# An encoder with a mixture of experts on one core: epsilon as a constant column, coefficient matmuls padded to full rows, the selector rounded by GpSimd, and the order of two waits

## The chip, the cores and the metric

The kernel runs on one core of a Trainium2 chip. The metric is the device time of one execution in microseconds (us). The engines are PE (TensorE, matmuls), DVE (VectorE), ACT (ScalarE), POOL (GpSimd) and SP (SyncE, here only for transfers). They run their own instruction lists in order and wait for each other through semaphores.

## The reference

There are 16 sequences of 256 tokens with 128 features. Each goes through the same work:

```
mod = silu(c) @ wmod                      # shifts, scales and gates, per sequence
h = layernorm(x) * (1 + ca) + sa
y = sqrt(128) * h + positions
for 4 layers:
    n = layernorm(y, ln1); q, k, v = n @ Wq + bq, n @ Wk + bk, n @ Wv + bv
    y = y + linear_attention(q, k, v) @ Wo + bo        # 16 heads of 8, elu + 1
    n = layernorm(y, ln2); y = y + relu(n @ W1 + b1) @ W2 + b2
x = x + ga * layernorm(y, lnf)
h = layernorm(x) * (1 + cb) + sb
coef = the two largest of softmax(h @ router), zero for the other six experts
x = x + gb * (sum over experts of coef * expert(h) + shared(h))
```

A layernorm divides by the root of the variance plus 1e-5. An expert is silu(h @ gate) * (h @ up) @ down with 64 hidden features. Everything is float32; the larger products are made of high and low parts in a rounded float32 format.

## The kernel before

**Chains.** Four sequences run at a time, as chains A, B, C and D, and four steps (loop variable `i`) do all 16. A chain's residual is `b.x`, 128 partitions of 2 tiles x 128 features. The pairs AB and CD run half a layer apart: in phase `n` of a step, one pair is in the attention half of a layer and the other in the feed-forward half. Phases 2 to 6 have the same shape; phases 7 to 9 also hold the end of the encoder, the routing and the experts, with the next step's first layer between them. The last step has no such neighbour.

**Order.** It is written out by hand, one list per engine. Each helper (`move`, `squares`, `rstd`, `scale`, `transposes`, ...) waits for the semaphores it needs and adds one to its own when it is done.

**The normalisation inside the encoder** (norms 1 to 9 of a chain). Weights are prepared so that the residual has mean zero, so the variance is the mean of squares. `move` (L941 to L947, DVE) adds a product from PSUM to `b.x`; it waits for PE's semaphore first and then for POOL's `biased`. `squares` (L406 to L416, ACT) squares each tile with a scale of 128^-0.5 and lets the accumulator sum it into `b.ms`. `rstd` (L646 to L656, POOL) adds epsilon to `b.ms`, giving `b.ve`, and raises that to -0.5, giving `b.rstd`. `scale` (L881 to L894, DVE) multiplies `b.x` by it into `b.xn` (127 of its 128 columns; the last is a constant 1). `transposes` (L1336 to L1342, PE) turns `b.xn`. The norms 0 and 10 use DVE's mean and variance `b.mv` instead, with the same `rstd`.

**The coefficients.** `route` (DVE) leaves two rounded parts of the eight coefficients, `b.parts`, 16 columns a tile. `coef_transposes` (L1440 to L1446, PE) makes 16 rows of them, `coefs` (L442 to L445, ACT) copies them as `b.coefT`, and `spread` (L1448 to L1454, PE) multiplies a slice of `sel_hi` with them, so that every hidden feature's row holds its expert's coefficient. `weigh` (L1038 to L1043, DVE) multiplies by that; it waits for the product before it and then for `spread`. Each chain does two transposes and two pairs of spread matmuls in a step.

**The start.** SP fetches the constants, the selector and the biases, then waits for the modulation. POOL's memsets, its transfers of `wo`, `w2` and the output biases, and four `rstd` come first in its list, then it waits for the modulation rows `M`. The selector `sel` is rounded into `sel_hi` by DVE at the end of its start list (`spreading_ones`, L831 to L833). `less_w2_means` (ACT) uses `eqk` of chain `l` as scratch for layer `l`.

All matmuls go through the helper on line 1305.

Of the kernel before, what the change touches and what calls it, by code (L numbers as in the profile page):

```python
# [39 lines left out]
P = 128  # L40
# [29 lines left out]
S_ROWS = PARTS * EXPERTS  # L70
SPREAD = (2, 2, 4, 8)
# [22 lines left out]
def selectors():  # L94

    k = np.zeros((S_ROWS, CH * P), np.float32)
    for c in range(CH):
        for m in range(P):
            k[2 * c + m // DE + EXPERTS * np.arange(PARTS), c * P + m] = 1
    return k  # L100
# [17 lines left out]
def program(nc, x_in, Wq, bq, Wk, bk, Wv, bv, Wo, bo, W1, b1, W2, b2, ln1_s, ln1_b, ln2_s, ln2_b, lnf_s, lnf_b,  # L118
# [3 lines left out]
    with ctx:  # L122
# [15 lines left out]
        sel_hi = sb("sel_hi", [S_ROWS, CH * P], F32R)  # L138
        sel = sb("sel", [S_ROWS, CH * P])
# [43 lines left out]
        for c in range(CHAINS):  # L183
# [3 lines left out]
            b.x = sb("x" + n, [P, TILES, D])  # L187
# [10 lines left out]
            b.zi = sb("zi" + n, [P, TILES, D])  # L198
# [26 lines left out]
            b.parts = sb("parts" + n, [P, TILES, PARTS, EXPERTS], F32R)  # L225
            b.coefT = sb("coefT" + n, [S_ROWS, T], F32R)
# [9 lines left out]
            b.s_rstd = sig("rstd", 2 * NORMS)  # L236
# [30 lines left out]
        A, B = AB  # L267

# [50 lines left out]
        def _(sync):  # L319
# [6 lines left out]
            sync.dma_start(sel[:, :], select).then_inc(s_sel, 16)  # L326
# [29 lines left out]
        def _(act):  # L356
# [49 lines left out]
            def squares(b, i, n):  # L406

                if n == 1:
                    act.wait_ge(b.s_centred.sem, b.s_centred.value(i, 2))
                else:  # L410
                    act.wait_ge(b.s_moved.sem, b.s_moved.value(i, n))
                for t in range(TILES):
                    unused = b.zi[:, t, :] if n == 1 else b.eq[:, t * P:(t + 1) * P]
                    last = act.activation(unused, b.x[:, t, :], ACT.Square, scale=float(D) ** -0.5,  # L414
# [27 lines left out]
            def coefs(b, i):  # L442
                act.wait_ge(b.s_eps.sem, b.s_eps.of(EXPERT_PS, "coefT", i))
                act.activation(b.coefT[:, :], b.ps[0:S_ROWS, 1, 0:T], ACT.Copy)\
# [36 lines left out]
            squares(a[1], 0, 2)  # L481
            less_w2_means(3, 4)
# [129 lines left out]
        def _(pool):  # L612
# [14 lines left out]
            pool.wait_ge(s_const, 10)  # L627
# [18 lines left out]
            def rstd(b, i, n):  # L646

                if 0 < n <= LAST:
                    pool.wait_ge(b.s_squares.sem, b.s_squares.value(i, n))
                    var = b.ms[:, :]  # L650
                else:
                    pool.wait_ge(b.s_moments.sem, b.s_moments.value(i, 1 if n == 0 else 2))
                    var = b.mv[:, :, 1]
                pool.tensor_tensor(b.ve[:, :], var, epsilon[:, :], ALU.add).then_inc(b.s_rstd.sem, 1)  # L654
                pool.wait_ge(b.s_rstd.sem, b.s_rstd.value(i, 2 * n + 1))
# [23 lines left out]
            rstd(f[1], 0, 0)  # L679
            pool.wait_ge(s_k, 32)  # L680
# [105 lines left out]
        def _(dve):  # L786
# [44 lines left out]
            def spreading_ones():  # L831
                dve.wait_ge(s_sel, 16)
                dve.tensor_copy(sel_hi[:, :], sel[:, :]).then_inc(s_ones, 1)  # L833

# [46 lines left out]
            def scale(b, i, n):  # L881

                dve.wait_ge(b.s_rstd.sem, b.s_rstd.value(i, 2 * n + 2))
# [57 lines left out]
            def move(b, i, n):  # L941

                ps = (b.s_wops, b.s_w2ps)[(n - 1) % 2]
                dve.wait_ge(ps.sem, ps.value(i, (n - 1) // 2 + 1))
                dve.wait_ge(b.s_biased.sem, b.s_biased.value(i, n + 1))
# [117 lines left out]
            dve.wait_ge(s_const, 10)  # L1063
# [38 lines left out]
            spreading_ones()  # L1102
# [200 lines left out]
        def _(pe):  # L1303
# [30 lines left out]
            pe.wait_ge(s_const, 10)  # L1334
# [105 lines left out]
            def coef_transposes(b, i):  # L1440
                pe.wait_ge(b.s_route.sem, b.s_route.value(i, b.s_route.per))
                pe.wait_ge(b.s_units.sem, b.s_units.of(EXPERT_UNITS, "product0", i))
                for t in range(TILES):
                    last = pe.transpose(b.ps[0:S_ROWS, 1, t * P:(t + 1) * P],
                                        b.parts[:, t, :, :].rearrange("p k e -> p (k e)").bitcast(F32), ident)
# [229 lines left out]
```

## Time and profile before

| | |
|---|---|
| median of 3 runs | 657.01 us (656.51, 657.01, 661.86) |
| the profiled execution | 657.81 us |
| its span, first to last instruction | 656.0 us |
| PE busy | 594.7 us, 91% of the span |
| DVE busy | 473.0 us, 72% |
| ACT busy | 380.4 us, 58% |
| POOL busy | 298.3 us, 45% |
| transfers in the first 16.4 us | 275 GB/s, the DMA engines 92% busy |
| mean granted TensorE clock | 0.966 of full; 0.61 from 16 to 66 us |

Busy time of one engine says little about the end, since the engines overlap. The chain of waits is followed back from the last instruction, at each step to what released it. The timeline lists instructions with their start and duration, and in brackets how long the engine was idle before and for whom. The ends of matmuls are modelled, so the pace of a row of matmuls is read from their starts.

### The profile page before, as it was taken

To read this page: it belongs to the slowest core of one execution; us is meant where nothing else is said; L and a number is where in the kernel's file an instruction comes from. 1 tells how busy PE (TensorE), PEld (TensorE's weight loads), DVE (VectorE), ACT (ScalarE), POOL (GpSimd) and SP (SyncE) were. 2 spreads that over 40 slices of the span, in tenths; PEclk is the share of its full clock that TensorE was granted. 3 is DMA by queue.
4 is the path that set the end of the run, shared out by engine and by line. 5 is a ranking of instruction groups with operands and counts; after the bars stand their busy time and mean duration, and the time that the engine had idled before them with its cause. 6 is when DMAs were issued, how large, how long until landed. Compare 5 with 4: busy or idle time off the path is not lost.

```text
span 656.0 us, 12768 instructions
## 1 busy us (share of the span) xinstructions
PE 594.7 (91%) x4378; PEld 538.4 (82%) x4378; DVE 473.0 (72%) x1441; ACT 380.4 (58%) x1344; POOL 298.3 (45%) x549
## 2 busy tenths in 40 slices
PE   2766999998999999997999999998999999998987
PEld 0255999997788999996788999997788999997776
DVE  6684666668997656669998565668998566668783
ACT  0657566654576665664576656664576665665431
POOL 5248544456443444455443354456443354445310
PEclk9566999999999999999999999999999999999999
DMA  9803300000000000000000000000000000000000
GB/s 275 289 3 101 121 2 1 1 1 1 1 16 18 0 1 2 1 1 0 2 17 11 8 1 1 1 2 0 2 17 2 17 1 2 1 1 1 1 16 17
DMA packets 10416, 15.79 MB, mean 24 GB/s; under 512 B 848, under 2 KB 7580, under 8 KB 10096
## 3 DMA queue, kind: packets, MB, share of 16 engines
q1 hardware_dynamic: 6192, 9.79, 4.7%
q0 software_dynamic: 1008, 2.83, 1.5%
q10 hardware_dynamic: 3152, 2.36, 1.3%
q8 instruction: 35, 0.57, 0.3%
q14 instruction: 29, 0.24, 0.1%
HBM read 12.84 MB, written 2.14 MB: 23 GB/s over the span
## 4 chain that ended last, share of the span: by engine, by line
PE 57%; DVE 17%; POOL 9%; ACT 9%; issue 5%; DMA 2%; DVEq 1%; SPq 0%; POOLq 0%
PE psC L1305 15%; PE psA L1305 15%; PE psD L1305 12%; PE psB L1305 9%; POOL rstdC L656 2%; POOL rstdA L656 2%; POOL rstdB L656 2%; ACT eqkA L414 1%; PE psB L1341 1%; ACT eqkC L414 1%; DVE xnB L886 1%; ACT eqkB L414 1%; PE psC L1341 1%; DVE xnA L886 1%; PE psA L1341 1%
## 5 line engine op out<-in xcount | busy, mean ns | idle before, releaser
L414 ACT ACTIVATE eqkC<-xC 128x128 f32<-128x128 f32 x64 | 19.3, 301 | 36.0 <-DVE xC L946 35.9
L654 POOL TENSOR_TENSOR veA<-msA,epsilon 128x2 f32<-128x2 f32 x36 | 7.0, 196 | 65.1 <-ACT eqkA L414 61.2
L656 POOL TENSOR_TENSOR rstdA<-veA,neghalf 128x2 f32<-128x2 f32 x44 | 33.6, 764 | 3.4
L656 POOL TENSOR_TENSOR rstdC<-veC,neghalf 128x2 f32<-128x2 f32 x44 | 33.6, 763 | 3.4
L654 POOL TENSOR_TENSOR veB<-msB,epsilon 128x2 f32<-128x2 f32 x36 | 7.3, 203 | 60.8 <-ACT eqkB L414 59.7
L654 POOL TENSOR_TENSOR veD<-msD,epsilon 128x2 f32<-128x2 f32 x36 | 7.1, 198 | 57.4 <-ACT eqkD L414 56.8
L654 POOL TENSOR_TENSOR veC<-msC,epsilon 128x2 f32<-128x2 f32 x36 | 7.1, 198 | 55.4 <-ACT eqkC L414 48.8
L656 POOL TENSOR_TENSOR rstdD<-veD,neghalf 128x2 f32<-128x2 f32 x44 | 30.7, 699 | 3.4
L656 POOL TENSOR_TENSOR rstdB<-veB,neghalf 128x2 f32<-128x2 f32 x44 | 30.6, 695 | 3.4
L1305 PE MATMUL psC<-w,H 128*128 128x128 f32 x256 | 31.5, 276 | 0.0
L1305 PE MATMUL psD<-w,H 128*128 128x128 f32 x256 | 31.4, 276 | 0.0
L1305 PE MATMUL psB<-w,H 128*128 128x128 f32 x256 | 31.4, 276 | 0.0
L1305 PE MATMUL psA<-w,H 128*128 128x128 f32 x256 | 31.2, 275 | 0.0
L414 ACT ACTIVATE eqkA<-xA 128x128 f32<-128x128 f32 x64 | 19.2, 301 | 20.5 <-DVE xA L946 20.5
L1305 PEld LDWEIGHTS psC<-w,H 128*128 128x128 f32 x256 | 30.0, 192 | 0.8 <-ACT H L435 0.7
L1305 PEld LDWEIGHTS psD<-w,H 128*128 128x128 f32 x256 | 30.1, 192 | 0.2
L1305 PEld LDWEIGHTS psA<-w,H 128*128 128x128 f32 x256 | 30.0, 192 | 0.0
L1305 PEld LDWEIGHTS psB<-w,H 128*128 128x128 f32 x256 | 29.8, 192 | 0.0
L435 ACT ACTIVATE H<-psD 128x512 f32<-128x512 f32 x32 | 19.0, 593 | 12.9 <-PE psD L1305 12.4
L1305 PE MATMUL psC<-xhiC,w_hi 128*128 128x256 f32 x64 | 20.9, 326 | 3.6 <-DVE xloC L909 3.6
L392 ACT ACTIVATE xhiB<-psB 128x256 fp32r<-128x256 f32 x32 | 12.4, 389 | 19.9 <-PE psB L1341 19.9
L414 ACT ACTIVATE eqkD<-xD 128x128 f32<-128x128 f32 x64 | 19.2, 305 | 7.9 <-DVE xD L946 7.4
(495 smaller groups left out, 2376.7 us busy)
## 6 DMA issues: line engine op xcount, KB each, us to landing
M<-modulation_rows SPq DMA_DIRECT2D x1, 2560.0 KB, 11.2
out<-X SPq DMA_DIRECT2D x16, 128.0 KB, 1.9
M<-modulation_rows SPq DMA_DIRECT2D x2, 640.0 KB, 5.3
M<-modulation_rows SPq DMA_DIRECT2D x1, 1280.0 KB, 8.8
M<-in_attn_W ACTq DMA_DIRECT2D x1, 1024.0 KB, 15.5
w<-in_attn_W POOLq DMA_DIRECT2D x1, 1024.0 KB, 11.6
X<-in_attn_x_in ACTq DMA_DIRECT2D x1, 512.0 KB, 4.7
wm<-in_wmod SPq DMA_DIRECT2D x1, 384.0 KB, 6.4
```

The source lines that it names most:

```text
L392: act.activation(b.x_hi[:, :], b.ps[:, n % 2, 0:T], ACT.Copy).then_inc(b.s_xT.sem, 1)
L414: last = act.activation(unused, b.x[:, t, :], ACT.Square, scale=float(D) ** -0.5, accum_out=b.ms[:, t:t + 1])
L435: act.activation(b.h[:, 2 * k:2 * k + 2, :], b.ps[:, k, :].rearrange("p (c t) -> p c t", t=T), ACT.Relu).then_inc(b.s_h.sem, 1)
L654: pool.tensor_tensor(b.ve[:, :], var, epsilon[:, :], ALU.add).then_inc(b.s_rstd.sem, 1)
L656: pool.tensor_tensor(b.rstd[:, :], b.ve[:, :], neghalf[:, :], ALU.pow).then_inc(b.s_rstd.sem, 1)
L886: dve.tensor_tensor(dst[:, :, 0:width], b.x[:, :, 0:width], b.rstd[:, :].unsqueeze(2).to_broadcast([P, TILES, width]), ALU.mult)\
L1305: return pe.matmul(o, lhsT, rhs, start=start, stop=stop)
L1341: last = pe.transpose(b.ps[:, n % 2, t * P:(t + 1) * P], src[:, t, :], ident)
```

## The change

It does five things.

- The residual of each chain becomes `b.xe` with 129 columns a tile; the last is the constant sqrt(128 x 1e-5). `squares` reads all 129, so that epsilon is in the sum, and `rstd` of norms 1 to 9 is the power alone. Its unused output goes to a 129-column view.
- `b.parts` becomes the first 16 of 128 columns, `b.columns`, the rest zero. The coefficient transposes, `b.coefT`, the selector and so the spread matmuls have 128 rows. The selector in memory has 128 rows, 112 of them zero.
- The selector is fetched into the `eqk` scratch of chain D and rounded by POOL after its four first `rstd`, no longer by DVE. ACT waits for that before `less_w2_means(3, 4)`.
- In `move` the two waits change places.
- POOL has eight more memsets in its start, and the engines wait for 18 instead of 10.

```diff
-            b.x = sb("x" + n, [P, TILES, D])
+            b.xe = sb("x" + n, [P, TILES, D + 1])
+            b.x = b.xe[:, :, 0:D]
...
-            b.parts = sb("parts" + n, [P, TILES, PARTS, EXPERTS], F32R)
-            b.coefT = sb("coefT" + n, [S_ROWS, T], F32R)
+            b.columns = sb("columns" + n, [P, TILES, S_ALL], F32R)
+            b.parts = b.columns[:, :, 0:S_ROWS].rearrange("p t (k e) -> p t k e", e=EXPERTS)
+            b.coefT = sb("coefT" + n, [S_ALL, T], F32R)
...
+        sel = flat(chains[3].eqk[:, :, :])
...
+        def rstds(n):
+            return n + 2 + (n > LAST)
...
-            sync.dma_start(sel[:, :], select).then_inc(s_sel, 16)
+            sync.dma_start(sel, select).then_inc(s_sel, 16)
...
+                unused = b.zie if n == 1 else flat(b.eqk[:, :, :])[:, 0:TILES * (D + 1)].rearrange(
+                    "p (t f) -> p t f", f=D + 1)
                 for t in range(TILES):
-                    unused = b.zi[:, t, :] if n == 1 else b.eq[:, t * P:(t + 1) * P]
-                    last = act.activation(unused, b.x[:, t, :], ACT.Square, scale=float(D) ** -0.5,
+                    last = act.activation(unused[:, t, :], b.xe[:, t, :], ACT.Square, scale=float(D) ** -0.5,
                                           accum_out=b.ms[:, t:t + 1])
...
-                act.activation(b.coefT[:, :], b.ps[0:S_ROWS, 1, 0:T], ACT.Copy)\
+                act.activation(b.coefT[:, :], b.ps[:, 1, 0:T], ACT.Copy)\
...
+            act.wait_ge(s_ones, 1)
             less_w2_means(3, 4)
...
                 pool.memset(b.v[:, :, D:], 1.0).then_inc(s_const, 1)
+                pool.memset(b.columns[:, :, S_ROWS:].bitcast(F32), 0.0).then_inc(s_const, 1)
+                pool.memset(b.xe[:, :, D:], float(np.sqrt(D * EPS))).then_inc(s_const, 1)
...
                 if 0 < n <= LAST:
                     pool.wait_ge(b.s_squares.sem, b.s_squares.value(i, n))
-                    var = b.ms[:, :]
-                else:
-                    pool.wait_ge(b.s_moments.sem, b.s_moments.value(i, 1 if n == 0 else 2))
-                    var = b.mv[:, :, 1]
-                pool.tensor_tensor(b.ve[:, :], var, epsilon[:, :], ALU.add).then_inc(b.s_rstd.sem, 1)
-                pool.wait_ge(b.s_rstd.sem, b.s_rstd.value(i, 2 * n + 1))
+                    pool.tensor_tensor(b.rstd[:, :], b.ms[:, :], neghalf[:, :], ALU.pow).then_inc(b.s_rstd.sem, 1)
+                    return
+                pool.wait_ge(b.s_moments.sem, b.s_moments.value(i, 1 if n == 0 else 2))
+                pool.tensor_tensor(b.ve[:, :], b.mv[:, :, 1], epsilon[:, :], ALU.add).then_inc(b.s_rstd.sem, 1)
+                pool.wait_ge(b.s_rstd.sem, b.s_rstd.value(i, rstds(n) - 1))
                 pool.tensor_tensor(b.rstd[:, :], b.ve[:, :], neghalf[:, :], ALU.pow).then_inc(b.s_rstd.sem, 1)
...
             rstd(f[1], 0, 0)
+            pool.wait_ge(s_sel, 16)
+            pool.tensor_copy(sel_hi[:, :], sel).then_inc(s_ones, 1)
             pool.wait_ge(s_k, 32)
...
-            def spreading_ones():
-                dve.wait_ge(s_sel, 16)
-                dve.tensor_copy(sel_hi[:, :], sel[:, :]).then_inc(s_ones, 1)
...
                 ps = (b.s_wops, b.s_w2ps)[(n - 1) % 2]
+                dve.wait_ge(b.s_biased.sem, b.s_biased.value(i, n + 1))
                 dve.wait_ge(ps.sem, ps.value(i, (n - 1) // 2 + 1))
-                dve.wait_ge(b.s_biased.sem, b.s_biased.value(i, n + 1))
...
-                    last = pe.transpose(b.ps[0:S_ROWS, 1, t * P:(t + 1) * P],
-                                        b.parts[:, t, :, :].rearrange("p k e -> p (k e)").bitcast(F32), ident)
+                    last = pe.transpose(b.ps[:, 1, t * P:(t + 1) * P], b.columns[:, t, :].bitcast(F32), ident)
```

## Rows read from the trace of the kernel before

**Rows 1.** The page, part 4: shares of the chain by engine.
```profile
PE 57%; DVE 17%; POOL 9%; ACT 9%; issue 5%; DMA 2%; DVEq 1%; SPq 0%; POOLq 0%
```
**Rows 2.** Timeline, one phase: start, duration, instruction, [idle before].
```profile
232.03 0.61 PE L1305 MATMUL psA<-wo,guA 128*128 128x128 f32 x4
...
232.68 0.43 DVE L946 TENSOR_TENSOR xA<-psA,xA 128x256 f32<-128x256 f32 x1 [0.84 <-PE psA L1305]
...
233.91 0.20 POOL L654 TENSOR_TENSOR veA<-msA,epsilon 128x2 f32<-128x2 f32 x1 [1.60 <-ACT eqkA L414]
...
234.18 0.90 POOL L656 TENSOR_TENSOR rstdA<-veA,neghalf 128x2 f32<-128x2 f32 x1
...
234.99 0.38 PE L1341 MATMUL psC<-K,xnC 128*128 128x128 f32 x2
235.12 0.42 DVE L886 TENSOR_TENSOR xnA<-xA,rstdA 128x254 f32<-128x254 f32 x1 [0.58 <-POOL rstdA L656]
...
235.60 0.44 PE L1341 MATMUL psA<-K,xnA 128*128 128x128 f32 x2 [0.23 <-DVE xnA L886]
...
235.88 0.42 DVE L909 TENSOR_TENSOR xloC<-psC,xhiC 128x256 fp32r<-128x256 f32 x1
...
236.56 0.28 PE L1305 MATMUL psC<-wqkv_hi,xloC 128*128 128x256 f32 x1
```
**Rows 3.** The chain in order of time: start, duration; first and last of 24.
```profile
71.25 0.92 POOL rstdC L656
...
586.71 0.92 POOL rstdA L656
```
**Rows 4.** Busy time by stretch: length, then PE, PEld, DVE, ACT, POOL.
```profile
295.00:312.00 17.00, 13.43 (x98) 11.69 (x99) 15.53 (x50) 6.61 (x26) 9.41 (x19) 1.00 0.00 0
```
**Rows 5.** Lines 654 and 656: count, ns min/median/max; one of four chains each.
```profile
L654 POOL TENSOR_TENSOR veA<-msA,epsilon x36: 188/196/201, 29.7 to 596.2; 128x2 f32<-128x2 f32 x36
...
L656 POOL TENSOR_TENSOR rstdA<-veA,neghalf x44: 691/702/917, 7.4 to 600.5; 128x2 f32<-128x2 f32 x44
```
**Rows 6.** Separate wait instructions of lines 945 and 1041; timeline, last step.
```profile
L945 DVEq EVENT_SEMAPHORE  x128: 21/21/21, 48.5 to 620.8; - x128
...
L1041 DVEq EVENT_SEMAPHORE  x32: 21/21/21, 171.2 to 646.0; - x32
...
644.43 0.50 PE L1305 MATMUL psD<-coefTD,sel_hi 16*128 16x256 f32 x2
...
645.04 0.69 DVE L1042 TENSOR_TENSOR H<-guD,psD 128x512 f32<-128x512 f32 x1 [1.49 <-PE psD L1305]
```
**Rows 7.** Timeline, DVE in the routing stretch.
```profile
320.79 0.94 DVE L886 TENSOR_TENSOR guD<-xD,rstdD 128x256 f32<-128x256 f32 x1
```
**Rows 8.** Timeline, PE in the routing stretch.
```profile
338.12 0.38 PE L1305 MATMUL psC<-kpC,wg 128*128 128x256 f32 x1
338.34 1.03 PE L1305 MATMUL psD<-kpD,wu 128*128 128x256 f32 x4
...
339.56 0.81 PE L1305 MATMUL psC<-kpC,wu 128*128 128x256 f32 x3
...
347.83 1.03 PE L1305 MATMUL psC<-kpC,wu 128*128 128x256 f32 x4
...
349.76 0.38 PE L1386 MATMUL psA<-K,attA 128*128 128x128 f32 x2
```
**Rows 9.** Timeline, the end of a step: DVE, ACT, POOL.
```profile
346.68 0.19 DVE L932 TENSOR_SCALAR denA<-psA 128x32 f32<-128x32 f32 x1 [0.28 <-PE psA L1305]
...
356.82 0.19 ACT L414 ACTIVATION_READ_ACCUMULATOR ziC<-xC 128x1 f32 x1
...
357.69 0.77 POOL L656 TENSOR_TENSOR rstdC<-veC,neghalf 128x2 f32<-128x2 f32 x1
```
**Rows 10.** Timeline, the start: DVE and POOL.
```profile
57.49 1.22 DVE L833 CAST sel_hi<-sel 16x512 fp32r<-16x512 f32 x1
...
23.47 0.72 POOL L669 TENSOR_TENSOR xA<-M,K 128x256 f32<-128x256 f32 x1 [12.53 <-DMA M<-modulation_rows]
```

More of the change, by code:

```diff
@@ L70 @@
 S_ROWS = PARTS * EXPERTS
+S_ALL = P
 SPREAD = (2, 2, 4, 8)
@@ L94, in selectors @@
 def selectors():
-    k = np.zeros((S_ROWS, CH * P), np.float32)
+    k = np.zeros((S_ALL, CH * P), np.float32)
     for c in range(CH):
@@ L137, in program @@
         pos = K[:, C_POS:C_POS + TILES * D].rearrange("p (t f) -> p t f", f=D)
-        sel_hi = sb("sel_hi", [S_ROWS, CH * P], F32R)
-        sel = sb("sel", [S_ROWS, CH * P])
+        sel_hi = sb("sel_hi", [S_ALL, CH * P], F32R)
         X = sb("X", [P, BATCH * TILES * D])
@@ L197, in program @@
             b.attT = b.gu[:, 1, :]
-            b.zi = sb("zi" + n, [P, TILES, D])
+            b.zie = sb("zi" + n, [P, TILES, D + 1])
+            b.zi = b.zie[:, :, 0:D]
             b.x_hi = sb("xhi" + n, [P, T], F32R)
@@ L235, in program @@
             b.s_squares = sig("squares", LAST)
-            b.s_rstd = sig("rstd", 2 * NORMS)
+            b.s_rstd = sig("rstd", NORMS + 2)
             b.s_normed = sig("normed", NORMS)
@@ L275, in program @@
         s_stored = sem("stored")
+        s_ones = sem("ones")
         s_const = sem("const")
         s_zero = sem("zero")
-        s_ones = sem("ones")
         s_parps = sem("parps")
@@ L626, in _ @@
                                a.rearrange("(a l) n -> a (l n)", a=1).to_broadcast([P, LAYERS * D])).then_inc(s_rest, 16)
-            pool.wait_ge(s_const, 10)
+            pool.wait_ge(s_const, 18)
             def moe_weights():
@@ L881, in scale @@
             def scale(b, i, n):
-                dve.wait_ge(b.s_rstd.sem, b.s_rstd.value(i, 2 * n + 2))
+                dve.wait_ge(b.s_rstd.sem, b.s_rstd.value(i, rstds(n)))
                 if 0 < n <= LAST:
@@ L1062, in _ @@
             fold_matrices()
-            dve.wait_ge(s_const, 10)
+            dve.wait_ge(s_const, 18)
             scale(a[0], 0, 0)
@@ L1101, in _ @@
             scale(a[1], 0, 2)
-            spreading_ones()
             for i in range(STEPS):
@@ L1333, in _ @@
             pe.wait_ge(s_low, 1)
-            pe.wait_ge(s_const, 10)
+            pe.wait_ge(s_const, 18)
             def transposes(b, i, n):
```

## The prediction

> **What bounds the kernel now.** I read the page first. TensorE (PE) is busy 91% of the span, but the chain of waits gives PE only 57%; VectorE (DVE), GpSimd (POOL) and ScalarE (ACT) have 35% of it [rows 1]. Each layer sends a chain through all four, and three kinds of stretch differ in what is last.
>
> In the **phases** PE is nearly full, with one hole in each. The timeline shows why: PE ends an output projection, DVE adds it (move), ACT squares, POOL adds epsilon, POOL takes the power, DVE scales, PE transposes. PE's pair of transposes for C starts at 234.99. A pair of 128-column fp32 matmuls passes in 0.22 here (two of 0.11), so A's pair could start at 235.21; it starts at 235.60, behind xnA [rows 2]. That hole of 0.39 us stands 24 times, six in each of four steps: the chain has 24 such powers with 0.91 to 0.93 us each, the first and the last shown [rows 3].
>
> In the **routing stretch** of a step PE has holes, and DVE is full: 15.53 of 17 us [rows 4]. At the **end** of the last step DVE idles for PE (1.49 us before one addition) [rows 6].
>
> **Epsilon in the squares.** Removed: 4 x 36 = 144 POOL additions, 0.20 us each [rows 5], with 0.07 of issue before the power (233.91 + 0.20, then 234.18): 0.27 off each chain. The additions that read mv stay. Added: a 129th element in 288 squares. No row shows it; bounds are nothing and a nanosecond or two. I take nothing, since the chain covers it no worse than now. A second effect: this power takes 0.90, the median is 0.702 [rows 2, 5], and beside it DVE begins xnC with two operands in SBUF. Begun 0.2 earlier it should be the 0.70 kind; bounds 0 and 0.2.
>
> **The two waits of move.** The late wait goes last in the source, and the trace shows the reverse of an aid. The compiled kernel has a separate semaphore instruction on line 945, 128 times: that is the second wait of the source, while the first sits on the addition. With the first one late, DVE starts 0.04 after PE's modelled end (232.03 + 0.61, then 232.68) [rows 2]. In weigh, too, the second wait (line 1041) is the separate one, and there it is late: PE's pair ends at 644.43 + 0.50 = 644.93, DVE starts at 645.04, 0.11 later [rows 6]. So the swap costs 0.07 wherever PE comes last. Behind it in DVE's queue stand scales and low parts, which move with it. Bounds 0 and 0.1.
>
> **A phase, summed.** Chain: -0.27 - 0.20 + 0.07 = -0.40. xnA starts at 234.72 and ends 0.42 later at 235.14, before PE comes for it at 235.21, so the hole closes. Then something else is late. The third matmul of C's projection needs xloC, which DVE starts at 235.88 after ACT's queue and ends at 236.30; that matmul stands at 236.56 now and could start at 236.34 [rows 2]: **0.22**. If the power stays at 0.90, xnA ends at 235.34, PE starts at 235.38, and it is 0.22 again. The move's 0.07 is inside that slack. 24 x 0.22 = **5.3 us**. Bounds: 0.05 a phase (a further wait right behind) and 0.39.
>
> **Routing, first half.** Three powers of this kind lie on the chain one after the other (chains B, B and D): 3 x 0.27. DVE's guD takes 0.94 where such an operation takes 0.42, because POOL's next addition holds it [rows 2, 7]; that addition also comes 0.27 earlier. Together 1.08. One of the four rests on an overlap and DVE is nearly full, so I take 0.8, four times: **3.2**. Bounds 0.3 and 1.2.
>
> **Coefficient matmuls with full rows.** From the first of four wu matmuls (347.83) to the transposes (349.76) PE does six fp32 matmuls of 256 columns and one pair of 16 rows: 1.93. The fp32 pace is 0.22 (338.12 to 338.34), which leaves 0.61, 0.3 each. The nearest stretch with full rows runs from four such matmuls at 338.34 to the next at 339.56 and has three rounded matmuls of 256 columns inside: 1.22 - 0.88 = 0.34, 0.11 each [rows 8]. Both kinds are fp32r; only the rows differ. So a pair goes from 0.61 to 0.23, near 0.4 less, 32 pairs, 12.2 us of PE. Most of it lies beside DVE's list and is worth nothing there. The 32 coefficient transposes get 128 columns of weights instead of 16, and the copies of coefT write the same 256 elements on more partitions: nothing, the load hides behind the matmul before it; without that cover the bound is 0.1 each.
>
> The Trainium skill speaks against this edit. TensorE: Matmul & The Clock Gate says (Part 2, step 1) that a weight load goes by columns while the row count does not matter, and its table of advice gives a single K=32 matmul the time of a K=128 one. By that the padding would bring nothing. The rows differ from it, and the sum goes by them.
>
> **Routing, second half** (three times, where a step follows). PE gains 0.8 with the first two pairs, and DVE can use part: it idles 0.28 for PE before denA (346.68), and 0.1 to 0.2 more before the weigh behind it. I take 0.47 for both; from there DVE's and ACT's lists run without a break. At their end ACT has C's squares at 356.82 + 0.19 = 357.01, and the last of four powers on POOL, queued behind four additions, starts at 357.69 [rows 9]. Without the additions it starts 0.07 after the squares, at 357.08: 0.61. Together 1.08, taken as 0.9: **2.7**. Bounds 0.4 and 1.5.
>
> **End.** Four pairs for C and D where DVE waits for PE: 4 x 0.4 = **1.6**. Bounds 0 and 2.5 (part of A's and B's pairs too).
>
> **Start.** DVE loses the selector's rounding, 1.22 at 57.49, on the chain [rows 10]; PE still has B's transposes before it, so I count 0.7 of it. Against that POOL rounds a 128x512 tile in a stretch where it idles 12.53 us before 23.47 [rows 10], so its own length is covered; but DVE's modulation steps lie there, and as guD shows, a DVE operation waits while POOL holds the port: up to the copy's whole length, 1.2. Without that idle time it would cost 1.2 on POOL as well. The memsets (some 900 elements a partition, I allow 0.4) come before POOL's weight transfers, and the selector is 256 KB, not 32, ahead of SP's bias transfers: 224 KB more at the 275 GB/s of the first slice is 0.8. Of this 2.4 I expect 0.7 to be seen, the rest hidden by the wait for the modulation rows. ACT's new wait stands late, long after the copy, and costs nothing; were the copy late, the fourth layer's weights and all of ACT's queue would be. Net **0**, bounds -1.1 (all of the rounding, none of the rest) and +1.7 (2.4 - 0.7).
>
> **Sum.** 5.3 + 3.2 + 2.7 + 1.6 = 12.8. The profiled execution took 657.81 (span 656.0), so **645.0**. That execution stands 0.8 above the median of 657.01, inside the spread of the three runs.
>
> **Rivals.** *Gains eaten (0.18).* Right behind each closed hole another wait is late, as xloC already is. Phases 24 x 0.05 = 1.2, routing 4 x 0.3 and 3 x 0.5, end 0.8: 4.7 less, 653.1. For it: DVE's full list. Against: in the phase I find 0.22 before the next wait.
>
> *The padding gives nothing (0.12).* The 0.4 belongs to something other than rows. Left are 5.3, 3.2 and 3 x 0.61: 10.3 less, 647.5. Against: the two stretches differ in nothing else that a row shows. This is the skill's rule at work.
>
> *All of it counts (0.08).* Upper bounds in the phases (9.4), in routing (4.8 and 4.5) and 1.6: 637.5.
>
> *The odd row, slower (0.06).* The residual's rows become 129 floats, so its second tile starts at byte 516, and every move, square, scale and POOL addition reads so. The phase's chain has four of them (move, square, square, scale): from 0.10 extra each the 0.40 is gone. At 0.15 a phase loses 0.2, 4.8 in all; in routing some 14 DVE operations a step on a full engine, 4 x 14 x 0.15 = 8.4; less the 7.5 from routing and end: 663.5. Against: the scale already writes 127 of each 128 elements and takes 0.42 like whole rows [rows 2].
>
> **Numbers.** The forecast's own case gets 0.56. Measurement tells about 1%, 6.6 us, from no change. Faster than 650.4 are the forecast, the padding's rival and the upper case, 0.76, less a little for their spread: 0.74; within 1% 0.19; slower 0.07. The range leaves out most of the upper case and the odd row, and takes in eaten gains: 639.5 to 653.5.
>
> **What the new profile should show.** No addition from ms; powers at 0.70 in the phases; nearly no wait before the transposes, and C's third matmul waiting instead; coefficient matmuls at 0.12; move starting 0.11 after PE's end; the rounding at 57.5 gone from DVE. Wrong would be: longer operations on x, phases as long as now, or a first phase that comes over 1 us later.

## The result

The kernel after took 639.92 us (median of 4 runs, 639.23 to 641.70), against 656.90 for the kernel before beside it: ratio 0.973 (0.970 to 0.975), 17 us faster. The forecast was 645.0, its range began at 639.5: the direction was right, the size 5 us too small. Repeated later with six runs it took 640.6, against 657.5.

The page of the kernel after, busy time by engine and the shares of the chain of waits; the second answers to [rows 1]:

```profile
PE 583.4 (91%) x4378; PEld 538.3 (84%) x4378; DVE 467.9 (73%) x1440; ACT 378.0 (59%) x1344; POOL 265.9 (42%) x414
...
PE 65%; DVE 15%; ACT 10%; issue 4%; POOL 3%; DMA 2%; DVEq 1%; SPq 0%; POOLq 0%
```

POOL fell from 9% to 3% of the chain and PE rose from 57% to 65%. Where did the 17.9 us between the two profiled spans (656.0 and 638.1) go? (By the medians it is 17.0: the profiled execution of the kernel before, 657.81, stands 0.9 above its median.) I cut both traces at the transposes of chain A (the pair psA<-K,xnA), which every phase has, and in each step at those between the two halves of a routing stretch. Differences to the kernel before, us; the columns "column alone" and "padding alone" are experiments, below:

```
stretch                                forecast   after   column alone   padding alone
start, to A's transposes of phase 2       0.0     -2.82      -0.22          +1.11
the phases (forecast for 24)             -5.3     -4.83      -5.22          -0.01
routing, first half, 3 times             -2.4     -4.23      -3.43          -0.50
routing, second half, 3 times            -2.7     -3.77      -0.86          -1.85
last step, from its routing on           -2.4     -2.22      -0.74          -1.33
sum                                     -12.8    -17.87     -10.47          -2.58
of it behind the start (the body)       -12.8    -15.05     -10.25          -3.69
```

The cuts leave 5 phases in the first step and 6 in each of the other three; the 24th lies in the start's row. Two terms are off: the start by 2.8 and routing by 2.9. The phases came 0.5 short and the last step 0.2, which leaves the 5.1. Of that 5.1, 0.9 is the profiled execution's distance from its median, from which the forecast was taken off; the bodies of two profiles of one kernel agree to 0.1, so nearly all of this 0.9 stands in the start's 2.8.

**A phase.** The timeline of the kernel after, the stretch of [rows 2]:

```profile
225.12 0.60 PE L1313 MATMUL psA<-wo,guA 128*128 128x128 f32 x4
...
225.84 0.43 DVE L955 TENSOR_TENSOR xA<-psA,xA 128x256 f32<-128x256 f32 x1 [0.92 <-PE psA L1313]
...
227.07 0.69 POOL L662 TENSOR_TENSOR rstdA<-msA,neghalf 128x2 f32<-128x2 f32 x1 [1.86 <-ACT eqkA L423]
227.21 0.41 DVE L895 TENSOR_TENSOR xnC<-xC,rstdC 128x254 f32<-128x254 f32 x1
...
227.79 0.42 DVE L895 TENSOR_TENSOR xnA<-xA,rstdA 128x254 f32<-128x254 f32 x1 [0.17 <-POOL rstdA L662]
...
228.08 0.38 PE L1349 MATMUL psC<-K,xnC 128*128 128x128 f32 x2
...
228.29 0.41 PE L1349 MATMUL psA<-K,xnA 128*128 128x128 f32 x2
...
228.97 0.42 DVE L918 TENSOR_TENSOR xloC<-psC,xhiC 128x256 fp32r<-128x256 f32 x1 [0.41 <-ACT xhiC L400]
...
229.50 0.34 PE L1313 MATMUL psC<-wqkv_hi,xloC 128*128 128x256 f32 x1
```

The addition is gone and the power takes 0.69. A's transposes follow C's by 0.21, so the hole of 0.39 is closed. Then C's third matmul waits for xloC: from the first output projection to that matmul it is 4.38 now and was 4.53. So of the hole's 0.39 a phase keeps 0.15 to 0.17, not the 0.22 of the working: xloC ends at 229.39 and the matmul starts 0.11 behind it, where the working had 0.04. The length of a phase says the same: from C's transposes to A's of the next phase it was 13.33 (234.99 to 248.32) and is 13.16 (228.08 to 241.24).

**Routing.** The operation that POOL held up for 0.94 [rows 7] takes 0.42. In the second half POOL's last power starts 0.07 behind ACT's squares (346.81 + 0.19), where it started 0.68 behind them [rows 9]; but DVE now waits for a product of PE:

```profile
311.99 0.42 DVE L895 TENSOR_TENSOR guD<-xD,rstdD 128x256 f32<-128x256 f32 x1
...
346.81 0.19 ACT L423 ACTIVATION_READ_ACCUMULATOR ziC<-xC 128x1 f32 x1
...
347.07 0.69 POOL L662 TENSOR_TENSOR rstdC<-msC,neghalf 128x2 f32<-128x2 f32 x1 [0.62 <-ACT ziC L423]
...
347.27 0.42 DVE L1058 TENSOR_TENSOR guC<-psC,M 128x256 f32<-128x256 f32 x1 [0.34 <-PE psC L1313]
```

**The start.** The granted clock (column behind the busy times; 0.50 is 1.2 GHz, 1.00 is 2.4) in slices of 4 us, the kernel before and then the kernel after:

```profile
56.00:60.00 4.00, 3.19 (x14) 2.49 (x13) 3.91 (x6) 2.26 (x8) 4.00 (x5) 0.50 0.02 4
60.00:64.00 4.00, 4.00 (x28) 4.00 (x27) 0.46 (x2) 1.32 (x4) 4.00 (x6) 0.72 0.84 256
```
```profile
56.00:60.00 4.00, 3.86 (x26) 3.57 (x25) 1.82 (x5) 2.68 (x10) 4.00 (x6) 0.73 0.37 86
60.00:64.00 4.00, 4.00 (x36) 4.00 (x35) 1.43 (x5) 2.74 (x7) 4.00 (x7) 1.00 0.88 313
```

PE's timeline shows the moment. Kernel before:

```profile
57.62 0.69 PE L1341 MATMUL psB<-K,xnB 128*128 128x128 f32 x2 [0.46 <-DVE xnB L886]
...
58.32 0.41 PE L1305 MATMUL psD<-wqkv_lo,xhiD 128*128 128x256 f32 x1
59.09 0.58 PE L1305 MATMUL psD<-wqkv_hi,xloD 128*128 128x256 f32 x1 [0.36 <-DVE xloD L909]
...
62.03 0.37 PE L1305 MATMUL psA<-xhiA,w_hi 128*128 128x256 f32 x1
62.24 0.28 PE L1305 MATMUL psA<-xhiA,w_lo 128*128 128x256 f32 x1
62.35 0.28 PE L1305 MATMUL psA<-xloA,w_hi 128*128 128x256 f32 x1
```

Kernel after:

```profile
56.37 0.69 PE L1349 MATMUL psB<-K,xnB 128*128 128x128 f32 x2
...
57.10 0.42 PE L1313 MATMUL psD<-wqkv_lo,xhiD 128*128 128x256 f32 x1
57.32 0.44 PE L1313 MATMUL psD<-wqkv_hi,xloD 128*128 128x256 f32 x1
...
58.00 0.36 PE L1313 MATMUL psD<-wqkv_hi,xloD 128*128 128x256 f32 x1
58.20 0.28 PE L1313 MATMUL psD<-xhiD,wqkv_hi 128*128 128x256 f32 x1
58.32 0.28 PE L1313 MATMUL psD<-xhiD,wqkv_lo 128*128 128x256 f32 x1
```

A matmul of 256 columns starts 0.21 after the one before it at half clock and 0.12 at full. That turn, the clock's rise, stands at 62.2 before and at 58.2 after. B's transposes come 1.25 sooner (57.62, 56.37), and of the 0.77 between the starts of D's second and third matmul (58.32 to 59.09) 0.22 is left.

### The profile page after: what moved, and what is told of

It reads as the page before. It is cut to its first block, busy times and chain, and to the rows that moved or that the text cites. A ratio compares the mean times of both kernels' runs of the same rounds, so it can differ in the third digit from the quotient of the medians.

```text
span 638.1 us, 12632 instructions
## 1 busy us (share of the span) xinstructions
PE 583.4 (91%) x4378; PEld 538.3 (84%) x4378; DVE 467.9 (73%) x1440; ACT 378.0 (59%) x1344; POOL 265.9 (42%) x414
## 4 chain that ended last, share of the span: by engine, by line
PE 65%; DVE 15%; ACT 10%; issue 4%; POOL 3%; DMA 2%; DVEq 1%; SPq 0%; POOLq 0%
PE psB L1313 15%; PE psD L1313 15%; PE psA L1313 15%; PE psC L1313 14%; PE psB L1349 2%; DVE xnB L895 1%; DVE H L1051 1%; PE psA L1349 1%; PE psC L1349 1%; ACT eqkB L423 1%; POOL rstdB L662 1%; DMA wm<-in_wmod 1%; ACT L431 1%; DVEq L885 1%; PE psD L1349 1%
## 5 line engine op out<-in xcount | busy, mean ns | idle before, releaser
L662 POOL TENSOR_TENSOR rstdA<-msA,neghalf 128x2 f32<-128x2 f32 x36 | 25.1, 697 | 68.8 <-ACT eqkA L423 64.9
L662 POOL TENSOR_TENSOR rstdB<-msB,neghalf 128x2 f32<-128x2 f32 x36 | 25.1, 698 | 68.6 <-ACT eqkB L423 67.2
L662 POOL TENSOR_TENSOR rstdD<-msD,neghalf 128x2 f32<-128x2 f32 x36 | 24.9, 692 | 64.6 <-ACT eqkD L423 63.4
L662 POOL TENSOR_TENSOR rstdC<-msC,neghalf 128x2 f32<-128x2 f32 x36 | 25.1, 697 | 59.9 <-ACT eqkC L423 52.2
L423 ACT ACTIVATE eqkC<-xC 128x129 f32<-128x129 f32 x64 | 19.4, 304 | 35.3 <-DVE xC L955 35.3
L423 ACT ACTIVATE eqkA<-xA 128x129 f32<-128x129 f32 x64 | 19.3, 303 | 22.0 <-DVE xA L955 22.0
L955 DVE TENSOR_TENSOR xA<-psA,xA 128x256 f32<-128x256 f32 x32 | 13.5, 423 | 13.9 <-PE psA L1313 13.9
L400 ACT ACTIVATE xhiB<-psB 128x256 fp32r<-128x256 f32 x32 | 12.4, 389 | 18.2 <-PE psB L1349 16.9
L423 ACT ACTIVATE eqkD<-xD 128x129 f32<-128x129 f32 x64 | 19.4, 312 | 6.4 <-DVE xD L955 6.4
L423 ACT ACTIVATE eqkB<-xB 128x129 f32<-128x129 f32 x64 | 19.2, 308 | 5.7 <-DVE xB L955 5.7
L918 DVE TENSOR_TENSOR xloC<-psC,xhiC 128x256 fp32r<-128x256 f32 x32 | 13.6, 424 | 10.7 <-ACT xhiC L400 10.5
## 6 DMA issues: line engine op xcount, KB each, us to landing
M<-modulation_rows SPq DMA_DIRECT2D x1, 2560.0 KB, 11.3
```

The source lines that it names most:

```text
L400: act.activation(b.x_hi[:, :], b.ps[:, n % 2, 0:T], ACT.Copy).then_inc(b.s_xT.sem, 1)
L423: last = act.activation(unused[:, t, :], b.xe[:, t, :], ACT.Square, scale=float(D) ** -0.5, accum_out=b.ms[:, t:t + 1])
L662: pool.tensor_tensor(b.rstd[:, :], b.ms[:, :], neghalf[:, :], ALU.pow).then_inc(b.s_rstd.sem, 1)
L918: dve.tensor_tensor(b.x_lo[:, :], b.ps[:, n % 2, 0:T], b.x_hi[:, :], ALU.subtract)\
L955: dve.tensor_tensor(b.x[:, :, :], b.ps[:, 0, 0:T].rearrange("p (t f) -> p t f", f=D), b.x[:, :, :], ALU.add).then_inc(b.s_moved.sem, 1)
```

## The experiments

Each was timed beside the kernel before on the same chip. The median of the kernel before was 656.9 beside the kernel after, 657.6 beside e1 to e4, 658.4 beside a1 to a4 and 657.5 to 657.9 beside the last group; so times of different groups are compared by their difference to it, and each such difference is known to 1 to 2.5 us. Single runs scatter by 3 us in the kernel after and by 6 in the kernel before (656.3 to 662.6). So I compare the bodies too, the profiled span from A's transposes of phase 2 on. Two profiles of the kernel after have 568.9 and 568.8.

### The parts alone, from the kernel before

**e1, the column.** All of the change's lines on `b.xe`, `zie`, `squares`, `rstds` and `rstd`, and no others:

```diff
-            b.x = sb("x" + n, [P, TILES, D])
+            b.xe = sb("x" + n, [P, TILES, D + 1])
+            b.x = b.xe[:, :, 0:D]
...
-                pool.tensor_tensor(b.ve[:, :], var, epsilon[:, :], ALU.add).then_inc(b.s_rstd.sem, 1)
+                    pool.tensor_tensor(b.rstd[:, :], b.ms[:, :], neghalf[:, :], ALU.pow).then_inc(b.s_rstd.sem, 1)
```


> The kernel before with the constant column alone: 129-column residual and squares, the power straight after the squares, coefficients, selector and waits as before. The theory after the result (each part is worth what its stretch of the two traces shows): 24 phases x 0.2 = 4.8 us, in routing about 0.7 before the first spread matmul and 0.3 at the end of a step, so 3 x 1.0, the last step 0.8, the start nothing: 8.6 less, about 648.4. Rival (holes close only together with the shorter spread pairs): phases as before the theory, routing nothing, about 652. Rival (the recorded sum of the prediction): 5.3 + 3.2 + 3 x 0.61 = 10.3 less, 646.7.

647.3 us, ratio 0.984 (0.982 to 0.986): 10.3 less. The theory's 8.6 missed; the prediction's terms gave the 10.3, but it is otherwise spread: first half 1.14 each, second half 0.29.

**e2, the padding.** 128 rows of columns, `coefT` and selector; DVE rounds.

```diff
-            b.coefT = sb("coefT" + n, [S_ROWS, T], F32R)
+            b.coefT = sb("coefT" + n, [S_ALL, T], F32R)
...
-                    last = pe.transpose(b.ps[0:S_ROWS, 1, t * P:(t + 1) * P],
+                    last = pe.transpose(b.ps[:, 1, t * P:(t + 1) * P], b.columns[:, t, :].bitcast(F32), ident)
```


> The kernel before with the padding alone (128-row coefT, selector and columns; the selector of 256 KB still rounded by DVE from its own buffer). Theory now: PE is what the routing stretch waits for around the spread pairs, so both pairs of a chain count: 0.4 less a pair, less about 0.5 given back once in the first half: 0.85 and 0.95, 1.8 x 3 = 5.4, and 1.4 in the last step: 6.8 less, about 650.2. Rival (the prediction's reading, most of the pairs lie beside DVE's list): 3 x 0.47 + 1.6 = 3.0, about 654. Rival (rows do not matter): 657.

653.2 us, ratio 0.994 (0.992 to 0.996): 4.4 less. The body is 3.7 shorter, near the prediction's 3.0 and not the theory's 6.8. Both parts alone give 10.25 + 3.69 = 13.9 in the body; together they give 15.05. So 1.1 belongs to neither alone.

**e3, the rounding.** POOL rounds the 16-row selector behind its first four `rstd`; DVE doesn't.

```diff
             rstd(f[1], 0, 0)
+            pool.wait_ge(s_sel, 16)
+            pool.tensor_copy(sel_hi[:, :], sel[:, :]).then_inc(s_ones, 1)
...
-            spreading_ones()
```


> The kernel before with one edit: the 16-row selector is rounded by POOL after its first four rstd instead of by DVE at the end of its start list. Theory now: the start's 2.8 us come from here, 0.7 to 1.2 as the rounding leaves DVE's chain at 57.5, the rest as TensorE's clock rises 3 to 4 us sooner: first transposes of C at about 69.5 instead of 72.7, 654.2. Rival (the prediction): 0.7, 656.3. Rival (the clock in the start comes from the memsets, the transfers or the waits of the other parts, not from here): 0 to 0.7 and the clock rows as before.

656.99 us, ratio 0.997 (0.994 to 0.999): 0.6 less, near the prediction's 0.7 and not the theory's 2.8. The wait in front of D's third matmul is gone, B's transposes come no sooner (57.66), the body is the same.

**e4, the waits of move.**

```diff
-                dve.wait_ge(ps.sem, ps.value(i, (n - 1) // 2 + 1))
                 dve.wait_ge(b.s_biased.sem, b.s_biased.value(i, n + 1))
+                dve.wait_ge(ps.sem, ps.value(i, (n - 1) // 2 + 1))
```


> The kernel before with the two waits of move in the other order and nothing else. Theory: DVE's move begins 0.11 instead of 0.04 us after PE's modelled end, 0.07 more on the phase's chain, where the phase's hole is still open: 24 x 0.07 = 1.7, some 658.5 with the routing. Rival (the order is worth nothing, the separate wait costs nothing when it is passed at once either way): 656.9. Rival (the swap helps, because the early wait no longer stands in the way): under 656.

656.8 us, ratio 1.000 (0.998 to 1.001). The 0.07 is there: where DVE waits for PE, `move` starts 0.38 behind the start of PE's last matmul, 0.31 before (median of the same 29 places in both traces). It isn't on the path: the phases are 0.15 shorter in sum, not 1.7 longer. (The body, 584.2 against 583.9, is longer only by a fall of the granted clock to half at 456.3 us in this profile, in a routing stretch that took 0.5 more.) The timeline of e4, a phase:

```profile
232.77 0.61 PE L1305 MATMUL psA<-wo,guA 128*128 128x128 f32 x4
...
234.87 0.41 DVE L886 TENSOR_TENSOR xnC<-xC,rstdC 128x254 f32<-128x254 f32 x1
234.99 0.83 POOL L656 TENSOR_TENSOR rstdA<-veA,neghalf 128x2 f32<-128x2 f32 x1
```

The power starts 0.07 later behind PE's projection than in [rows 2] (2.22 instead of 2.15) and takes 0.83 instead of 0.90: it ends 3.05 behind it in both. Its end stays with DVE's xnC, which starts 2.10 behind the projection in both, and not with its own start.

### The parts taken out of the kernel after

**a1, 16 rows again.**

```diff
-S_ALL = P
+S_ALL = 16
```


> The kernel after with the padding alone undone: columns, coefT, the selector and the transposes have 16 rows again. Theory (what the padding is worth beside the epsilon column, from the traces of the kernel after and of the column alone): first halves 3 x 0.27, second halves 3 x 0.97, last step 1.5: 5.2 more, 645.1. Rival (it is worth what it was worth alone, 4.4): 644.3. Rival (the prediction's term, 3 x 0.47 + 1.6 = 3.0): 642.9.

646.8 us, ratio to before 0.982 (0.978 to 0.985). The body is 573.9 against 568.9: 5.0, the theory's 5.2 (first halves 0.27, second 0.97, last step 1.5).

**a2, DVE rounds again.**

```diff
-            pool.tensor_copy(sel_hi[:, :], sel).then_inc(s_ones, 1)
...
+                dve.tensor_copy(sel_hi[:, :], sel[:, :]).then_inc(s_ones, 1)
```


> The kernel after with the selector (128 rows) fetched into its own buffer and rounded by DVE at the end of its start list. Theory: the hole of 0.55 before D's third matmul at 57 us comes back, and each matmul that then still runs at half clock is lost twice: 0.6 to 1.5 more, 640.5 to 641.4 in the median, and single runs differ by up to 2 us as the clock's rise falls. Rival (the start's 2.8 us are all this edit's): 642.7. Rival (nothing): 639.9.

642.9 us, ratio 0.975 (0.972 to 0.978). The body is 0.2 longer, the profile's start 2.4; by the table below only 0.3 of that is the hole. 642.9 lies near the rival's 642.7, but the kernel before took 1.5 more here than beside the kernel after. By the difference to it (15.5 less, against 17.0) the edit costs 1.5, the upper end of the theory.

**a3, the old order of move's waits.**

```diff
-                dve.wait_ge(b.s_biased.sem, b.s_biased.value(i, n + 1))
                 dve.wait_ge(ps.sem, ps.value(i, (n - 1) // 2 + 1))
+                dve.wait_ge(b.s_biased.sem, b.s_biased.value(i, n + 1))
```


> The kernel after with move's two waits in the order of before. DVE's move should start 0.07 sooner behind PE. Theory: in the kernel after the power no longer ends by DVE's port (there the 0.07 vanished), so it is on the chain, but the phase's hole is closed and C's third matmul waits behind xloC: about 0.02 a phase, 24 x 0.02 = 0.5 less, 639.4, phases at 1.34 instead of 1.2 less than before per six. Rival (hidden): 639.9. Rival (all of the 0.07 counts): 24 x 0.07 = 1.7 less, 638.2.

640.8 us, ratio 0.972 (0.969 to 0.975). The body is 0.2 shorter over the whole run: the phases gain 5.0 instead of 4.8. Nearly all of the 0.07 is hidden. It took 17.6 less than the kernel before, the kernel after 17.0 and 16.9: no difference clear of the noise.

**a4, additions back.**

```diff
+                pool.tensor_tensor(b.ve[:, :], var, epsilon[:, :], ALU.add).then_inc(b.s_rstd.sem, 1)
+                pool.wait_ge(b.s_rstd.sem, b.s_rstd.value(i, 2 * n + 1))
```


> The kernel after with the epsilon column alone undone: 128-column residual, POOL adds epsilon before each power. Theory (the column is worth what it was alone, 10.3): 650.2, phases back to 13.95 us per pair of phases, the power at 0.83 to 0.90 there. Rival (less, since in the routing stretch padding and column share one hole): 8.5 more, 648.4.

653.4 us, ratio 0.991 (0.987 to 0.994). The body is 580.2, that of e2 (580.3), so beside the padding the column is worth 11.3, not 10.3. Neither theory had it more than alone.

### How many rows

```diff
-S_ALL = P
+S_ALL = 64      # and 96
```


> The kernel after with columns, coefT, the selector and the transposes at 64 rows. If the pace of a spread matmul goes with the rows, a pair stands between the 0.61 of 16 rows and the 0.23 of 128, about 0.4, and the second half of a routing stretch loses about half of 0.97; if only full rows are quick, a pair takes 0.6 again and it loses all of it; if anything above 32 rows is quick, nothing is lost.

> The kernel after with 96 rows. With 64 rows the second half of a routing stretch lost 0.98 against 128 rows, as much as with 16 (0.97). If only full rows are quick it is 0.97 again; if the bound lies above 64, nothing to 0.5.

The stretch from the four wu matmuls to the transposes, 1.93 in [rows 8]. In order: the kernels after, with 96, and with 64 rows.

```profile
337.93 1.03 PE L1313 MATMUL psC<-kpC,wu 128*128 128x256 f32 x4
338.60 0.59 PE L1313 MATMUL psD<-coefTD,sel_hi 128*128 128x256 f32 x2
...
339.46 0.38 PE L1394 MATMUL psA<-K,attA 128*128 128x128 f32 x2
```
```profile
338.46 1.03 PE L1313 MATMUL psC<-kpC,wu 128*128 128x256 f32 x4
339.14 0.59 PE L1313 MATMUL psD<-coefTD,sel_hi 96*128 96x256 f32 x2
...
340.00 0.38 PE L1394 MATMUL psA<-K,attA 128*128 128x128 f32 x2
```
```profile
340.88 1.03 PE L1313 MATMUL psC<-kpC,wu 128*128 128x256 f32 x4
341.83 0.50 PE L1313 MATMUL psD<-coefTD,sel_hi 64*128 64x256 f32 x2
...
342.80 0.38 PE L1394 MATMUL psA<-K,attA 128*128 128x128 f32 x2
```

1.53, 1.54 and 1.92: a pair costs 0.4 less at 96 and 128 rows than at 64 and 16. The bodies say the same: 568.9 and 569.0, against 573.7 and 573.9. The 64-row and the 96-row kernel have one run each (645.8 and 640.5), which says little alone.

The weight loads (PEld) show more. The last load of the wu matmuls and the pair's own, the kernel before and then the kernel after:

```profile
348.27 0.19 PEld L1305 LDWEIGHTS psC<-kpC,wu 128*128 128x128 f32 x1
348.79 0.29 PEld L1305 LDWEIGHTS psD<-coefTD,sel_hi 16*128 16x128 f32 x2 [0.33 <-issue]
```
```profile
338.36 0.19 PEld L1313 LDWEIGHTS psC<-kpC,wu 128*128 128x128 f32 x1
338.57 0.41 PEld L1313 LDWEIGHTS psD<-coefTD,sel_hi 128*128 128x128 f32 x2
```

With full rows the pair's first load follows 0.21 behind the one before it, as in a row of equal matmuls; with 16 rows 0.52 behind it, and with 64 rows too. The load itself takes the same: 0.18 us with 16 and 64 rows, 0.19 with 128. That is what the Trainium skill states (TensorE: Matmul & The Clock Gate, Part 2, step 1): the time of a weight load goes by the columns, not by the rows, and the trace agrees. The rival that the prediction made of it, that the padding gives nothing, is false here; with few rows the load only starts later. Whether the few rows bring this, or the change from full rows to few and back, no run separates, since these pairs always stand among matmuls with full rows.

### The start and the clock

**w1 and w2: ten idle products** in PE's wait before the first transposes of phase 1, in the kernels after and before. **w0** is the kernel after itself.

```diff
             pe.wait_ge(s_folded, 2 * LAYERS)
+            for k in range(10):
+                mm(chains[2].ps[:, 1, 0:T], ident, K[:, 0:T])
```


> The kernel after with ten fp32 products of 256 columns more, whose results nobody reads, in PE's wait of 4.75 us before the first transposes of phase 1 (50.0 to 54.7 us). Theory (the start is long because PE runs at half clock from 55 us until it rises, at 58.2 to 63.7 us in the eight kernels seen): the rise comes 2 to 5 us sooner, and each us of it gives back half a us: 1 to 2.5 less than the same kernel without, 637.5 to 639; from run to run less scatter. Rival (that stretch waits for DVE and ACT, the clock is by the way): 640 as before, the rise sooner and holes in PE in its place.

> The kernel before with the same ten idle products at the same place. Theory (clock): the rise, seen at 62.0 us in the profile of before, comes at 56 to 60: 1 to 3 less, about 655; and against the kernel after with the ten products the difference is then the body's 15.1 us (from the first transposes of phase 2 on) plus 0.9 before phase 1 and 0.55 for the rounding's hole: 16.5, so that 1.3 of the 2.8 us of the start are the clock's. Rival (the start's 2.8 have another cause in the change): the difference stays at 17.9.

> The kernel after itself, unchanged, so that its median comes from the same chip and hour as the two before it in this call. Theory: the four runs on record (639.2 to 641.7) had an early rise of the clock; 640.5 here, 17 less than before in the same call. Rival: 639.9.

w1 640.0 us (639.5 to 640.3), w0 640.6 (638.9 to 641.9), w2 656.6 (655.6 to 658.3); ratios 0.973 (0.970 to 0.975), 0.974 (0.971 to 0.976) and 0.998 (0.996 to 0.999). In w1 the clock rises at 53.5 and stays; the products overshoot, the transposes come at 56.4 instead of 55.3, and still nothing is lost. The median gains 0.6, less than the theory's 1 to 2.5; the scatter shrinks from 3.0 to 0.8. (w0 came as expected, 16.9 less than the kernel before.) Between w2 and w1 lie 16.6: the 16.5 of w2's theory, and not the rival's 17.9. In w2's profile the clock rose at 52.7, fell at 59.5 and rose again at 62.9. Before it fell, PE had been idle for 1.07 before B's transposes and then stood idle for 0.80 before D's third matmul. That profile is of the slowest of w2's twelve runs (658.3, mean granted clock 0.974, median of the twelve 0.987), so most of them may not have had the fall; the windows of w2:

```profile
56.00:58.00 2.00, 1.30 (x8) 0.64 (x7) 1.75 (x3) 1.97 (x10) 1.97 (x2) 1.00 0.00 0
58.00:60.00 2.00, 0.83 (x5) 0.62 (x5) 2.00 (x4) 1.01 (x4) 2.00 (x3) 0.88 0.00 0
60.00:62.00 2.00, 2.00 (x10) 2.00 (x11) 0.79 (x3) 0.66 (x2) 2.00 (x3) 0.50 0.35 113
```

**w3 and w4: five such products**, in the kernel after and in e3's.

```diff
+            for k in range(5):
```


> The kernel after with five idle products instead of ten, so that they end (at half clock 4.3 us behind 50.3) before the transposes that wait for DVE. Theory (clock): the rise comes at 53 to 55 us as with ten, the first transposes stand at 55.3 instead of 56.4, and half to all of that 1.1 is gained over the 640.0 with ten: 639.0 to 639.5, scatter under 1 us. Rival (five are too few to raise the clock before the stretch): 640.6 as without them, scatter of 3 us.

> The kernel before with the selector rounded by POOL (no hole at 58 us, in which the clock fell again in the kernel before with ten idle products: it rose at 52.7, was back at half from 59 and rose at 62.8) and five idle products. Theory (the start's 2.8 us are the hole and the clock): with both gone the difference to the kernel after with five is the body's 15.1 and 0.9 before phase 1: 655.0 if that one takes 639.0. Rival (something else of the change shortens the start): it stays near 657.

w3 639.7 us (638.6 to 641.8), ratio 0.973 (0.971 to 0.975); w4 657.4, ratio 0.998 (0.997 to 1.000). The difference is 17.7, where the theory that the hole and the clock make up the start had 16.0; w3's own theory missed too (639.0 to 639.5, scatter under 1; it was 3.2). So the two pairs disagree: 16.6 with ten products, 17.7 with five. Each is known to some 1.5 us, so they don't settle what the hole and the clock are worth together. Two things are seen in the profiles. B's transposes come at 57.90 in w4 and at 56.16 in w3. And w4 has full clock from 54.4 to 57.8, then half, and rises again at 61.3, while w3 has it from 51.9 on and keeps it, though PE idled as long in w3 (1.40 and 0.75) as in w4 (0.97 and 1.07). The longer of w3's waits:

```profile
54.42 0.44 PE L1349 MATMUL psD<-K,xnD 128*128 128x128 f32 x2 [1.40 <-DVE xnD L895]
```

What brought the clock down in w4 and not in w3 is therefore not shown.

All kernels side by side: start of B's transposes in phase 1, the clock's rise behind them, A's transposes of phase 2, the time between first and third, and the body, in us. "Worked out" is 12.82 (r64) plus 0.46 for each us of half clock beyond r64's 1.79; 0.46 is the slope from r64 to a1, (13.92 - 12.82) / (4.19 - 1.79).

```
kernel             B      rise   A, ph.2  between  worked out   body
before           57.62   62.24   72.05    14.43     14.12      583.9   DVE rounds
e1 column        56.45   63.19   71.83    15.38     15.09      573.7   DVE rounds
e2 padding       58.70   63.33   73.16    14.46     14.13      580.3   DVE rounds
e4 waits         57.82   63.72   72.85    15.03     14.71      584.2   DVE rounds
a2               57.44   61.59   71.67    14.23     13.91      569.1   DVE rounds
e3 POOL rounds   57.66   60.06   70.71    13.05     13.10      583.7
after            56.37   58.20   69.23    12.86     12.84      568.9
w0 after again   56.54   58.99   69.66    13.12     13.12      568.8
a1 16 rows       57.15   61.34   71.07    13.92     13.92      573.9
a3 old order     57.03   60.98   70.82    13.79     13.81      568.7
a4 additions     58.06   62.76   72.11    14.05     14.16      580.2
r64              57.41   59.20   70.23    12.82     12.82      573.7
r96              56.47   59.11   69.66    13.19     13.21      569.0
w1, w3           56.88, 56.16: full clock    12.60, 12.62      568.8
```

Three things can be read. The clock's rise falls anywhere from 58.2 to 63.7, and each us of half clock costs 0.46; the slope comes from two kernels, and the others without DVE's rounding lie within about 0.1 of it. Where DVE rounds, the stretch is 0.29 to 0.33 longer than that. And with full clock from the first matmul (w1, w3) it takes 12.6, not the 12.0 of the slope: the first matmuls on D still start 0.22 to 0.23 apart there. So the kernel after's own 12.86 leaves only 0.25 to gain.

## Why the prediction came out 5 us short

**Start, forecast 0, measured -2.82.** (By the medians it is 1.8 to 1.9: 17.0 and 16.9, less the bodies' 15.05 and 15.17.) This step failed most: the prediction put the start at a net of nothing. By the table: B's transposes 1.25 sooner; 2.79 us less of half clock at 0.46, which is 1.28; and the hole 0.31 at most. That makes 2.8. I counted the hole (as 0.7) and set it against the cost of POOL's copy, the memsets and the larger transfer. B's transposes came no later by them in e3 (57.66, with POOL's copy) and sooner in the kernel after; only e2, with memsets and transfer, has them later (58.70), in the profile of its slowest run. I had left out two things. First, the additions stand in the start's chain too. From DVE's addition to B, 50.67, to B's transposes, 57.62, it is 6.95; in e1 6.36 (50.09 to 56.45). Two additions with their issue stood there; the kernel before, then e1:

```profile
54.08 0.20 POOL L654 TENSOR_TENSOR veD<-msD,epsilon 128x2 f32<-128x2 f32 x1 [0.63 <-ACT ziD L414]
54.36 0.69 POOL L656 TENSOR_TENSOR rstdD<-veD,neghalf 128x2 f32<-128x2 f32 x1
55.01 0.20 POOL L654 TENSOR_TENSOR veB<-msB,epsilon 128x2 f32<-128x2 f32 x1
55.28 0.77 POOL L656 TENSOR_TENSOR rstdB<-veB,neghalf 128x2 f32<-128x2 f32 x1
```
```profile
53.51 0.69 POOL L658 TENSOR_TENSOR rstdD<-msD,neghalf 128x2 f32<-128x2 f32 x1 [1.26 <-ACT ziD L421]
54.16 0.69 POOL L658 TENSOR_TENSOR rstdB<-msB,neghalf 128x2 f32<-128x2 f32 x1
```

Second, PE is full from B's transposes on and at half clock, so the moment of the rise is worth us, and I held the clock constant. How much of the earlier rise the change brings isn't settled: e1, with sooner transposes, had one of the latest rises, 63.2. Over the six profiles with the column, POOL's rounding and no idle products the rise stands at 58.2 to 61.3, over the five where DVE rounds at 61.6 to 63.7, and over the two where POOL rounds without the column at 60.1 (e3) and 62.8 (a4). That B's transposes come sooner is the column's, by all profiles without idle products: 56.4 to 57.4 in the eight profiles with it, 57.6 to 58.7 in the five without. The remaining 0.6 of B's 1.25, before 50 us, isn't taken apart.

**Routing, first half, 0.8 taken, 1.41 measured.** This step failed next. The working had found 1.08 (three powers and the held guD) and cut it by a quarter because DVE was nearly full. e1 measured 1.14: the full sum counts. The other 0.27 is the padding, which I had hidden beside DVE's list (0.02 to 0.25 alone).

**Routing, second half, 0.9 taken, 1.25 measured.** The padding was given 0.47 and the additions 0.61. e1 shows 0.29 for the additions, since behind the power DVE waits for C's product, in its guC; e1's timeline:

```profile
351.77 0.69 POOL L658 TENSOR_TENSOR rstdC<-msC,neghalf 128x2 f32<-128x2 f32 x1 [0.62 <-ACT ziC L421]
...
352.35 0.42 DVE L1056 TENSOR_TENSOR guC<-psC,M 128x256 f32<-128x256 f32 x1 [0.71 <-PE psC L1312]
```

That wait of 0.71 is 0.34 in the kernel after. The padding is worth 0.62 alone and 0.97 beside the column: each part hid some of the other's gain (0.29 + 0.62 alone, 1.25 together), as is to be expected if POOL's additions and PE's pairs end nearly together. Three times that 0.34 is nearly all of the 1.1 that neither part has alone.

**Phases, 5.3 and 4.8.** The mechanism was right: power at 0.69, all 24 holes closed (the second pair of transposes starts 0.22 behind the first, 0.61 before), xloC next. The size came near by luck. A phase keeps 0.17, not 0.22 (in the median 13.34 before and 13.17 after, from the first pair of transposes of one phase to that of the next), which is 4.1 for 24. The row reaches 4.83 because in each step its last cut, and not its first, stands behind a hole: four whole holes of 0.39 are counted in it, part of which is given back behind the cut, in the routing. The 0.4 between e1 (5.22) and the kernel after lies in the first phase behind each routing: from A's transposes to A's it is 13.08 in e1, a1 and the 64-row kernel, 13.25 in the kernel after and 13.24 with 96 rows. So it goes with the padding, three times 0.17, which has gained 0.97 just before.

**The two waits.** The 0.07 is exact (0.31 to 0.38) and its worth zero, the lower bound. **Padding.** The pair fell by 0.4 as worked out (1.93 to 1.53). **Last step.** 2.4 forecast, 2.2 measured. **Rivals.** The odd row costs nothing in `move` (0.43 as before) and nearly nothing in the squares (0.31 and 0.29 as before). The upper case came nearest, for its routing terms (4.8 and 4.5).

None of the versions beats the kernel after clear of the noise: ratios 0.972 (a3), 0.973 (w1) and 0.973 (w3) against 0.973 and 0.974, with intervals that overlap.

## What to carry to other kernels

When two engines end a stretch nearly together, a gain on one is worth less alone than beside a gain on the other: sum the parts of a change along the joint path, and don't discount each for the other's cover. When an operation is taken off a chain, look for every place where that chain stands, the start too. In a start, read the granted clock before you call a stretch neutral: here each us of half clock under a full PE cost 0.46 us, and its rise moved by 5.5 us between the profiles. And a total that comes out near the forecast doesn't show that its terms do: look at one phase.

## What the runs showed of the hardware that I had not expected

- Rounded 256-column matmuls with 16 or 64 rows: a pair costs 0.4 us more than with 96 or 128 (1.92 against 1.54 for the same stretch). The load takes the same, but starts 0.52 behind the load before it instead of 0.21.
- The granted clock rises at another time of the program from run to run: the same kernel had it at 58.2 and at 59.0 us. It fell from full to half at 59.5 us in w2, after idle times of PE of 1.07 and during one of 0.80, and stayed full in w3 through 1.40 and 0.75.
- A POOL power that starts just behind the start of a DVE `scale` (two SBUF operands) ends 0.55 behind the end of that operation, in the kernel before and in e4: it is 0.90 long when it starts 0.05 behind it, 0.83 when 0.12, 0.77 when 0.20, and 0.69 when it starts first (kernel after).
